# Expert outputs written to DRAM in tile order and gathered back per token, instead of scattered per tile

## The reference, cut to what matters

```
logits = h @ wg
topv, topi = jax.lax.top_k(logits, TOP_K)          # TOP_K = 4 of 16 experts
gate = jax.nn.softmax(topv, -1)
weights = jnp.zeros_like(logits).at[bidx, sidx, topi].set(gate)
a = silu(einsum('bsd,edh->bseh', h, w1)) * einsum('bsd,edh->bseh', h, w3)
y = einsum('bseh,ehd->bsed', a, w2)
moe = einsum('bsed,bse->bsd', y, weights)
return x + moe
```

## Time and profile before

| | us |
|---|---|
| median of 3 runs | 793.95 (793.32 to 794.41) |
| profiled execution, first to last instruction (span) | 827.0 |
| in it: tile loop, from the first gather (644.64) to the end of the last `weigh` (802.88) | 158.2 |
| in it: the end, from there to the end of the span | 24.1 |
| POOL busy in the whole span | 461.6 |
| PE busy in the whole span | 622.4 |

### The profile page before, as it was taken

One profiled execution on the slowest core, in us unless ns is written; L12 is line 12 of the kernel. 1 busy time (PEld: TensorE's weight loads), 2 busy tenths in 40 slices (PEclk: granted clock), 3 DMA queues, 4 the chain that ended last, 5 costly groups with the idle time before them and its releaser, 6 DMA issues.

```text
span 827.0 us, 16334 instructions
## 1 busy us (share of the span) xinstructions
PE 622.4 (75%) x5400; PEld 423.1 (51%) x5400; DVE 570.0 (69%) x1932; ACT 436.9 (53%) x1213; POOL 461.6 (56%) x422
## 2 busy tenths in 40 slices
PE   0367997578888557789999998997768877777760
PEld 0133665356656444466666766766643444444540
DVE  5999558788888779677786886785558433444445
ACT  4833442177877513575766676666621455555540
POOL 1041753188897713686986995774321565655630
PEclk9758998779999968899999999999997899999995
DMA  9400131224744600240423223224036222222327
GB/s 296 177 1 1 52 102 47 81 77 154 229 152 128 217 1 0 52 78 14 91 55 87 40 50 55 52 40 166 1 139 260 63 90 73 87 81 82 88 61 254
DMA packets 83467, 78.05 MB, mean 94 GB/s; under 512 B 49408, under 2 KB 75776, under 8 KB 82880
## 3 DMA queue, kind: packets, MB, share of 16 engines
q1 hardware_dynamic: 78880, 64.39, 26.8%
q0 software_dynamic: 4512, 12.71, 5.2%
HBM read 47.53 MB, written 18.55 MB: 80 GB/s over the span
## 4 chain that ended last, share of the span: by engine, by line
PE 33%; DVE 27%; ACT 12%; issue 11%; POOL 9%; another core or an unknown queue 3%; DMA 2%; SPq 1%; DVEq 0%; ACTq 0%; POOLq 0%
PE ps L1826 5%; ACT arena L1063 5%; PE ps L2118 5%; PE ps L2024 4%; PE ps L2040 3%; DVE arena L1514 3%; PE ps L2141 2%; PE ps L1883 2%; PE ps L2007 2%; ACT arena L979 2%; POOL arena L837 2%; POOL arena L831 1%; PE ps L2130 1%; PE ps L1750 1%
## 5 line engine op out<-in xcount | busy, mean ns | idle before, releaser
L1063 ACT ACTIVATE arena<-arena,tiny 128x128 f32<-128x128 f32 (+1 forms) x256 | 113.2, 443 | 45.8 <-DVE tiny L1514 45.7
L837 POOL TENSOR_TENSOR arena<-arena,tiny 128x512 f32<-128x512 f32 x64 | 93.8, 1466 | 56.5 <-DVE tiny L1526 56.4
L1522 DVE COPY arena<-ps 128x512 f32<-128x512 f32 x64 | 44.2, 690 | 57.1 <-PE ps L2007 56.8
L2024 PE MATMUL ps<-arena 128*64 128x128 f32 x768 | 56.1, 279 | 27.1 <-ACT arena L1049 15.2
L1514 DVE CUSTOM_DVE_ANT_0 arena<-ps,causal 128x128 f32<-128x128 f32 (+1 forms) x256 | 75.9, 352 | 0.5 <-issue 0.5
L878 POOL DMA_INDIRECT y_store<-arena x47 | 46.4, 988 | 53.4 <-DVE arena L1685 47.3
L2118 PE MATMUL ps<-arena 128*128 (+1 forms) x282 | 68.6, 379 | 7.6 <-issue 7.5
L1826 PE MATMUL ps<-arena,xt_hi 128*128 128x512 f16 (+1 forms) x224 | 64.2, 372 | 7.9 <-DVE xt_lo L1286 3.7
L2024 PEld LDWEIGHTS ps<-arena 128*64 128x64 f32 x768 | 41.8, 136 | 49.5 <-issue 36.0
L872 POOL DMA_INDIRECT arena<-h_store,arena x47 | 46.0, 980 | 33.9 <-DVE arena L1645 19.9
L1659 DVE SCALAR_TENSOR_TENSOR ps<-ps,arena 128x256 f32<-128x256 f32 x47 | 20.3, 432 | 61.8 <-ACT arena L1115 44.6
(11 more groups left out here) (295 smaller groups left out, 1709.7 us busy)
## 6 DMA issues: line engine op xcount, KB each, us to landing
e_store<-arena SPq DMA_DIRECT2D x13, 768.0 KB, 4.3
arena<-e_store SPq DMA_DIRECT2D x13, 768.0 KB, 9.8
work<-w_dram SPq DMA_DIRECT2D x27, 256.0 KB, 4.6
xn<-w_dram SPq DMA_DIRECT2D x21, 256.0 KB, 4.7
arena<-w_gate_up_t_dram SPq DMA_DIRECT2D x2, 1024.0 KB, 9.0
arena<-wq_dram SPq DMA_DIRECT2D x2, 1024.0 KB, 8.2
arena<-wo_dram SPq DMA_DIRECT2D x2, 1024.0 KB, 5.6
work<-y_store SPq DMA_DIRECT2D x8, 256.0 KB, 5.6
```

Of the source, the lines that this page charges most:

```text
L837: nc.gpsimd.tensor_tensor(p, p, arec[:, u % 4, :].unsqueeze(2).broadcast_to([P, GH, L]), ALU.mult)\
L1063: nc.scalar.activation(p, p, ACT.Exp, bias=anm[:, u % 4, h:h + 1], scale=-1.0, accum_out=asum[:, u % 4, h:h + 1]).then_inc(a_exp, 1)
L2024: last = mm(ps[half * HD:(half + 1) * HD, 5, pair * P:(pair + 1) * P], av[b % 2][:, k, g * HD:(g + 1) * HD], apt[:, u % 2, k, h * P:(h + 1 ...
```

## The change

The scatter per tile goes away. `y_store` becomes 47 tiles of 128 rows in tile order, and SP stores each finished tile by one plain transfer of 128 KB (L687 of the changed kernel), as soon as DVE has made it. The trash area, its iota and `index` go away, and `source` takes one DVE instruction in place of five. A new table `back` holds, for each token, the four rows of `y_store` in which its outputs lie (`four` minus 1, one DVE instruction). POOL gathers the rows back by it: 32 indexed transfers, one for each of 8 token groups and 4 choices (`take_back`, L873). The four of group 0 come between the last gathers of the loop, since all rows of the first 128 tokens lie in the first 16 tiles; the other 28 follow once all 47 stores have landed. DVE adds and SP stores per token group, 32 additions of 128x256 and 8 stores of 128 KB, in place of 16 additions of 128x512 and 4 stores of 256 KB. PE and ACT run the same instructions as before.

```
-            for i in range(YBUF):
-                sp.wait_ge(y_sent[i], 16 * len(range(i, TILES, YBUF)))
-            for b in range(B):
-                for i, dst in enumerate(y_back):
-                    rows = y_store[GROUP_AT[i] + b * S:GROUP_AT[i] + (b + 1) * S, :]
-                    sp.dma_start(dst[:, b * TB:(b + 1) * TB, :], rows.rearrange("(t p) d -> p t d", p=P))\
-                        .then_inc(fetched[1 + b], 16)
+            for i in range(TILES):
+                sp.wait_ge(y_ready, i + 1)
+                sp.dma_start(y_store[i * P:(i + 1) * P, :], y[:, i % YBUF, :]).then_inc(y_sent[i % YBUF], 16)
...
-            def send(i):
-                pool.wait_ge(y_ready, i + 1)
-                nc.gpsimd.indirect_dma_start(y_store, bass.IndirectOffsetOnAxis(index[:, i:i + 1], 0),
-                                             y[:, i % YBUF, :], None).then_inc(y_sent[i % YBUF], 16)
+            def take_back(t, j):
+                at = t * TOP_K + j
+                nc.gpsimd.indirect_dma_start(y_back[j][:, t, :], None, y_store if t else y_store[0:NE * P, :],
+                                             bass.IndirectOffsetOnAxis(back[:, at:at + 1], 0))\
+                    .then_inc(landed(t)[0], 16)
...
-            for i in range(TILES):
-                if i + AHEAD < TILES:
-                    gather(i + AHEAD)
-                send(i)
+            for i in range(TILES - AHEAD):
+                gather(i + AHEAD)
+                if i == BACK_AT[0]:
+                    for k in range(YBUF):
+                        pool.wait_ge(y_sent[k], 16 * len(range(k, NE, YBUF)))
+                if i in BACK_AT:
+                    take_back(0, BACK_AT.index(i))
+            for k in range(YBUF):
+                pool.wait_ge(y_sent[k], 16 * len(range(k, TILES, YBUF)))
+            for t in range(1, T):
+                for j in range(TOP_K):
+                    take_back(t, j)
...
+            nc.vector.tensor_scalar(back.rearrange("p (t j) -> p t j", j=TOP_K), four, 1.0, None, ALU.subtract)
...
-            vec.wait_ge(trash_made, 1)
-            nc.vector.tensor_scalar(signed, found, 0.0, -1.0, ALU.is_gt, ALU.mult)
-            link(nc.vector.scalar_tensor_tensor(empty, found, 0.0, trash_ids, ALU.is_equal, ALU.mult))
-            link(nc.vector.tensor_tensor(source, signed, found, ALU.add))
-            link(nc.vector.tensor_scalar(source, source, TOKENS - 1, None, ALU.bitwise_and))
-            nc.vector.scalar_tensor_tensor(index, empty, 2.0 * TOKENS, found, ALU.add, ALU.add).then_inc(index_ready, 1)
+            nc.vector.tensor_scalar(source, found, 1.0, 0.0, ALU.subtract, ALU.max).then_inc(index_ready, 1)
...
+            for t in range(T):
+                vec.wait_ge(*landed(t))
+                for j, src in enumerate(y_back):
+                    last = nc.vector.tensor_tensor(x[:, t, :], x[:, t, :], src[:, t, :], ALU.add)
```

More of the change, by code:

```diff
@@ L58 @@
 HROW = 2 * D + 2 * NE
-YROWS = TOKENS * TOP_K + 1 + TILES * P
-GROUP_AT = (TOKENS * 2 + 1, TOKENS * 3 + 1, TOKENS, 0)
+BACK_AT = (NE + 5, NE + 7, NE + 9, NE + 11)
 GBUF = 8
@@ L315, in build @@
         one_tile = c6([T * TOP_K, TILES], F16)
[L316 to L319, removed]
+        back = c6([T * TOP_K], I32)
         source = c6([TILES], I32)
@@ L462, in build @@
         home_ready = sem("home_ready")
-        trash_made = sem("trash_made")
+        first_back = sem("first_back")
         rows_in = [sem(f"rows_in{i}") for i in range(GBUF)]
@@ L481, in build @@
         h_store = nc.dram_tensor("h_store", (TOKENS, HROW // 2), F32, kind="Internal").ap()
-        y_store = nc.dram_tensor("y_store", (YROWS, D), F32, kind="Internal").ap()
+        y_store = nc.dram_tensor("y_store", (TILES * P, D), F32, kind="Internal").ap()
         block = top.enter_context(nc.Block())
@@ L572, in stage_wait, with landed @@
             eng.wait_ge(stage_loaded[i % 2], 16 * sum(FW_DMAS[i % 2:i + 1:2]))
+        def landed(t):
+            if t == 0:
+                return first_back, 16 * TOP_K
+            return rows_in[t], 16 * (len(range(t, TILES, GBUF)) + TOP_K)
         def raw_buffer(n):
@@ L682, in _ @@
             sp.dma_start(h_store.rearrange("(t p) c -> p t c", p=P), hrow.bitcast(F32)).then_inc(h_stored, 16)
-            for i in range(YBUF):
-                sp.wait_ge(y_sent[i], 16 * len(range(i, TILES, YBUF)))
-            for b in range(B):
-                for i, dst in enumerate(y_back):
-                    rows = y_store[GROUP_AT[i] + b * S:GROUP_AT[i] + (b + 1) * S, :]
-                    sp.dma_start(dst[:, b * TB:(b + 1) * TB, :], rows.rearrange("(t p) d -> p t d", p=P))\
-                        .then_inc(fetched[1 + b], 16)
-            outs = out.rearrange("(t p) d -> p t d", p=P)
[L691 to L695, removed]
+            for i in range(TILES):
+                sp.wait_ge(y_ready, i + 1)
+                sp.dma_start(y_store[i * P:(i + 1) * P, :], y[:, i % YBUF, :]).then_inc(y_sent[i % YBUF], 16)
+            outs = out.rearrange("(t p) d -> p t d", p=P)
+            for t in range(T):
+                sp.wait_ge(total_ready, t + 1)
+                sp.dma_start(outs[:, t, :], x[:, t, :]).then_inc(stored, 16)
+            sp.wait_ge(stored, 16 * T)
         CONSTS = 12 * 16
@@ L860, in _ @@
             pool.wait_ge(src_ready, 10)
-            nc.gpsimd.iota(trash_ids, pattern=[[P, TILES]], base=2 * TOKENS + 1, channel_multiplier=1)\
-                .then_inc(trash_made, 1)
             for c in range(2):
@@ L1696, in _ @@
                     split_act(i)
[L1697 to L1702, removed]
+            for t in range(T):
+                vec.wait_ge(*landed(t))
+                for j, src in enumerate(y_back):
+                    last = nc.vector.tensor_tensor(x[:, t, :], x[:, t, :], src[:, t, :], ALU.add)
+                    if j < TOP_K - 1:
                         link(last)
@@ L2193, in inputs_for @@
     token = p[:, None, None] + P * np.arange(T)[None, :, None]
-    route[:, 337:369] = (token + np.array((1, 1 + TOKENS, -TOKENS, -2 * TOKENS))).reshape(P, T * TOP_K)
+    route[:, 337:369] = np.broadcast_to(token + 1, (P, T, TOP_K)).reshape(P, T * TOP_K)
     route[:, 97:113] = 1 + P * np.arange(NE)
```

## The result

The changed kernel takes 812.69 us (median of 4 runs, 810.96 to 815.62), the kernel before 793.63 beside it (4 runs, 792.95 to 794.41): a ratio of 1.0238 with an interval of 1.0215 to 1.0262. It is 19.1 us slower. The profiled execution of the changed kernel has a span of 810.6 us and took 812.68 in all.

What follows compares the result with a forecast made beforehand. The prediction took the loop to be bound by latency, no engine full, and the end by a chain of waits. Index arithmetic -0.6, loop 0 and end +19.6 made +19.0 on 793.95: 813 us, range 787 to 823.

Steps and rivals of the forecast that it cites:

- The stalls belong to that one execution, the timed runs don't have them: Tile loop: 24 ACT and DVE waits on "remote", 31.1 us, belong to the profiled execution; timed runs hardly have them.
- my estimate of the profiled span, 815: Whole changed kernel under the profiler: span may fall to 827.0 - 30.8 + 19.0 = 815 while timed runs get slower.
- Index arithmetic, -0.6: Before the first gather: one instruction in place of five saves 0.8 us, the new `back` adds 0.2.
- The loop, 0 with bounds of -1.6 and 0: Tile loop: gains 0, since seven tiles gathered ahead and four `y` buffers cover POOL's 0.04 us lag per tile.
- The early gathers fit: Tile loop: group 0's four gathers, 5 us of POOL over eight tiles, fit into time the sends leave.
- The end, +19.6: After the last finished tile: store, 28 gathers at 1.253 us, additions, last store take 43.7 us instead of 24.1.
- The sum: Whole kernel: -0.6 + 0 + 19.6 = +19.0 us on the median of 793.95, giving 813.
- Faster through the loop: Rival, tile loop: timed runs have the stalls too, loop gains 30.8 us against 19.0 lost: 782; chance 0.21.
- A shorter step: Rival, gathers at the end: without the 0.30 us gap before each, 805; chance 0.08.
- Additions that hold up gathers: Rival, the end: DVE's two-input additions and POOL's gathers exclude each other, 824; chance 0.09.
- the price of 10.8 us: At the end: 24 additions of 0.45 us in series with the gathers, 10.8 us more.
- the only sign for that rival in the earlier trace: Loop start: first gather took 1.55 us beside a two-input DVE addition, the next 0.96; a long wait might also explain it.

Runs made afterwards that it cites:

- e1: Changed kernel's loop (plain stores, no scatters) without its four early gathers, with the end of the kernel before; rows read back in tile order: 791.84 us, ratio 0.9971.
- before_again: The kernel before, unchanged, profiled a second time: span 793.8 us, 795.6 in all.
- e3: Changed kernel, with the 28 gathers at the end fetching rows of 512 bytes in place of 1 KB: 813.2 us, ratio 1.0241.
- e4: Changed kernel with 14 gathers at the end in place of 28, the 32 additions kept: 795.31 us, ratio 1.0002.
- e2: Changed kernel with a scatter per tile kept on POOL, into tile order, in place of SP's plain store: 819.16 us, ratio 1.0316.
- e6: Kernel before, but each tile's scatter adds to a DRAM array, then copied to the output; no reads back or DVE additions: 882.69 us, ratio 1.112.

## Why the prediction was right

The forecast was 813 and the measurement 812.69. The mechanism was right: a chain of gathers at POOL's own pace behind the last tile. That the number agrees to 0.3 us is luck, since single terms of the sum are off by 0.4 to 1.4 us and cancel. The steps, in the prediction's order:

*The stalls belong to that one execution, the timed runs don't have them.* Right, and it decided the forecast: e1 shows the loop without scatters at 791.84, not 763. The reason that I gave was wrong: I put the stalls down to the profiler ("would bear out that the stalls were the profiler's"), and eight later profiles, before_again among them, have none. With it goes my estimate of the profiled span, 815; it was 810.6.

*Index arithmetic, -0.6.* Right as far as the first gather, and not beyond it in this trace. From the first instruction on `found` to the first gather pass 1.10 us in the changed kernel (640.40 to 641.50) and 1.93 in before_again (642.57 to 644.50), 0.83 less; what the new `back` costs earlier was not measured by itself. But to the first finished tile it is 14.19 us against 13.82, 0.37 more. PE runs 18 matmuls that only keep it busy (`keep_busy`) before it turns to the gathered rows. In the changed kernel they end at 647.1, after the rows of the first two tiles have come (644.9 and 646.2); in before_again they end at 647.7, before those of the second tile have (649.2). First the changed kernel, then before_again:

```profile
640.19 6.92 PE L1749 MATMUL ps<-ident_bf 128*128 128x512 bf16 x18
642.36 5.30 PE L1750 MATMUL ps<-ident_bf 128*128 128x512 bf16 x18
```

The granted clock is 0.50 (1.2 GHz) from 640.2 to 646.0 us in the first and 0.52 from 642.4 to 645.0 in the second, and 0.99 and 1.00 (2.4 GHz) behind that. It had been 1.00 from 626.0 to 635.8 in the first, with PE busy for 8.2 of these 9.8 us, and 0.50 from there on. The prediction has no term for this. The traces of e3 and e4 show it too (14.18 and 14.17), that of e1 does not (12.96); how often the timed runs have it is open.

*The loop, 0 with bounds of -1.6 and 0.* This term was mis-sized: it is 111.8 against 113.2, so -1.4. I had worked out that POOL falls 0.04 us a tile behind, and then took it that the seven tiles gathered ahead cover this. They do until late in the loop; then single steps of 3.1 us appear. That rows come late is seen directly only in e2, where POOL is further behind; for the kernel before it is not shown.

*The early gathers fit.* Right, by the two loops of equal length.

*The end, +19.6.* It is 44.2 against 24.2: +20.0. Piece by piece: the plain store lands after 1.69, where I took 2.4 from the scatter and 0.14 for SP's wake; POOL wakes after 0.84 (766.41 + 1.69 to 768.94), where I took 0.3, so that the two errors partly cancel (2.56 to the first gather against 2.84); 1.259 a step against 1.253; landing 2.78 against 2.80; additions 1.8 as said; and from the last addition (807.11 + 0.43) to the end of the span 3.1 against 2.5.

*The sum.* With 0.4 up to the first tile it is 0.4 - 1.4 + 20.0 = 19.0, with -0.8 it is 17.8; measured is 19.1, with 17.1 to 20.8 by the interval of the ratio (0.0215 and 0.0262 of 793.6). Both lie within it, and single traces cannot close the account further: the first instruction on `found` comes at 640.40, 640.72 and 642.25 us in the changed kernel, e3 and e4, which have the same code up to there.

*The rivals.* Faster through the loop: e1 rules it out. A shorter step: the 0.30 in front of each gather stayed, whatever was fetched (e3) and however many (e4).

Additions that hold up gathers: the mechanism is there, the price of 10.8 us is not. 28 gathers at 1.259 instead of 1.253 leave 0.2 us for all of it. It is one gather, at 786.44, which took 1.18 and began 0.06 us into the addition of 786.38; the others took 0.94 or 0.95. Across the five kernels with gathers at the end, seven of those gathers took more than 1.0 us (1.05 to 1.19). All seven began 0.06 to 0.19 us into an addition, as the one at 778.18 in e4 did, and each lost what was left of that addition less 0.13 us. Gathers that began 0.3 us or more into one lost nothing (783.60 in e4), nor did those that began at most 0.04 us into one, whose addition took 0.47 to 0.49 in place of 0.43. The rows look as if a gather does something about 0.13 us after its start that cannot run beside such an addition; that is a reading of these numbers, not shown by itself.

The Trainium skill's rule ("SBUF — State Buffer", section "Who interferes with whom") says that an addition with two SBUF inputs and a POOL operation that reads SBUF shut each other out. These rows agree with it near the start of a gather, and only there: the gather at 785.19 took 0.95 although two additions began while it ran, from 785.47 on. The Trainium skill's page adds, as an inference, that descriptor writing needs the other interface, which fits this last row. The prediction's price took each addition as a loss in series; in the changed kernel 23 of the 28 gathers do not begin beside one.

The first gather of the loop, the only sign for that rival in the earlier trace rows, takes 1.56 in the changed kernel too, and there too it begins beside a two-input addition:

```profile
641.22 0.68 DVE L1649 TENSOR_TENSOR arena<-arena 128x496 f32<-128x496 f32 x1
641.50 1.56 POOL L867 DMA_INDIRECT arena<-h_store,arena  x1 [18.68 <-DVE arena L1645]
```

It is so in the traces of all kernels here, before and before_again included (1.51 to 1.56), while the first gather after the long wait at the end (768.94) begins beside none and takes 0.94. So the long wait is not what makes it long, and the addition may be. But 0.40 us of the addition were left and 0.61 was lost, so that the rest is open.

## What to carry to other kernels

Moving indirect transfers from a loop to the end trades a price that is hidden for one that is paid in full: here 28 gathers x 1.25 us behind the last tile, against 47 scatters beside matrix work that cost 1.4 us of loop and 1.3 us between the last tile and the first read. Before you move one, count the instructions of the engine that issues it in the new place, not the bytes. And compare the span of a trace with the timed median first: where they differ by 4%, look for the stretch that differs, or take a second trace, before a stall in it is counted as something to be won.

## What was not expected of the hardware

- A plain store of 128 KB to DRAM lands 1.69 us after its issue (the last one of the changed kernel), the scatter of the same bytes 2.43 (before_again).
- An indirect transfer of 128 rows holds POOL for 0.94 us at 512 bytes a row and 0.95 at 1 KB, and 0.30 more pass before the next one starts (e3 and the changed kernel).
- A gather that starts 0.06 to 0.19 us into a two-input addition of DVE takes 1.05 to 1.19 us; one that is under way when such an addition starts takes its usual 0.95.
- A scatter that adds holds POOL for 1.55 to 1.64 us, and most land 3.7 to 3.9 after their issue (e6).
- One profiled execution of the kernel before had a span 33 us above the median of its timed runs, with 24 waits on "remote" in the loop and none elsewhere; the second profile of the same kernel and all others have none.
